# Moving the normalised row-pass input and its mean term from GpSimd to VectorE

## The chip, the cores and the metric

The kernel runs on one core of a Trainium2 chip. The metric is the device time of one execution in microseconds (us). Three runs of the kernel before gave 5276.94, 5283.10 and 5283.75 us, median 5283.1 us. Differences under about 0.2% (10.6 us) can't be told from no change.

## The reference

The input `x` has 8 batches of 128 channels of 128x128 images, float32. Two layers follow each other. Each adds its result to its input, and each first normalises over groups of 4 channels (mean and variance over the 4 images of a group):

```python
def _gn(v, G=32, eps=1e-5):
    g = v.reshape(B_, G, C_ // G, H_, W_)
    m = jnp.mean(g, axis=(2, 3, 4), keepdims=True)
    s = jnp.var(g, axis=(2, 3, 4), keepdims=True)
    return ((g - m) / jnp.sqrt(s + eps)).reshape(v.shape)

x = x + _L0_conv_ref(_gn(x), L0_conv_f)      # per image: upsample by 2 with 12 taps (rows, columns),
                                             # leaky ReLU (slope 0.01), filter and downsample by 2
x = x + _L1_conv_ref(_gn(x), ...)            # rfft2, keep 64x64 modes at both ends, contract with
                                             # four complex factors a, b, c, d, irfft2
```

## The kernel before

Work is cut into quads: the 4 images of one normalisation group, `[128 rows, 4 images, 128 columns]`. There are 256 quads, and four quads make a half, the unit of loading and of the statistics (64 halves). Stage one (`phase1`) does the first layer and the row and column transforms of the second; it fills the first 2840 us of the span. Stages two and three (`phase2`, `phase3`) contract the modes and transform back. The change touches stage one alone.

In stage one every engine runs the same list of steps, one step per quad, each in its own hand-written order, with semaphores between the engines. The loop body has 8 steps (`body`, L605 to L611 on ScalarE, L808 to L814 on VectorE), so the step's place in the half is q mod 4, and after every 32 quads `spectra` is put in. In what follows "place 1" is a step with q mod 4 = 1. At step q:

- TensorE (L385 to L454): `up_cols` of images 0 and 1 (column upsampling, f16 pairs), `down_rows` of quad q-1, at place 2 also `x_sums` (statistics of the next half, L335), then `tails` (L362, the edge columns of both directions; it waits for `e_yb` and `e_yc`), `up_rows` of quad q+1, first half (L324, reads the normalised input `g` and waits for `g_ok`), `up_cols` of image 2 and 3, `up_rows` second half, `down_cols` and `row_transform`.
- ScalarE (L530): copies `L` (slope times the PSUM tile), the high halves of `A`, `Y` and `Z`, and the square root of the variance.
- VectorE (L694): in order `yf(0)`, `yf(1)` (L704, the leaky ReLU as a maximum), `y_tail` (L691, writes `Yc` from the two SBUF tiles `Yt` and `mask`), statistics of `x1b` (L714), the low halves of `Z` and `Zt`, `Ytf`, at place 2 `stats_copy` (L639), `a_low` (L684), `yf(2)`, `yf(3)`, at places 0 and 1 `x_stats` (L632, statistics of two quads of the next half), `a_low` second half, at place 2 `stats_out` (L647, reciprocal of the deviation, `rstd`), and last the new `x1b` (L749).
- GpSimd (L270): high half of `Y` for image 0 (L276), low halves of images 0 and 1 (L283), `Yt` low (L289), at place 2 `variance` (L255), high half of image 2, low halves of images 2 and 3 (L283), and last `ground(q + 2, k + 2, half)` (L240), which makes `g` for quad q+2: `g = x * rstd - nmr`. On the first quad of a half it waits for `rstd` and makes `nmr`, the mean over the deviation, first (L245). `g` has two buffers.

A wait on `e_yc` in `tails` is thus answered by `y_tail`, which is the third instruction of VectorE's step, right behind the last two instructions of its step before (`a_low`, `x1b`).

The lines of TensorE's step on which the argument rests:

```python
if down:
    pe.wait_ge(e_yb, 2 * q)
    pe.wait_ge(e_yc, q)
...
tails(e, o, pr[3], up, down)
if nxt:
    pe.wait_ge(g_ok, q + 2)
    pe.wait_ge(e_yf, 4 * q + 1)
    up_rows(q + 1, k + 1, 0, pr[4])
```

Of the kernel before, what the change touches and what calls it, by code (L numbers as in the profile page):

```python
# [52 lines left out]
def wait(eng, sem, n):  # L53

    if isinstance(n, int) and n <= 0:
        return
    eng.wait_ge(sem, n)  # L57
# [16 lines left out]
def carry(eng, carried):  # L74


    eng.sem_inc(carried, 1)


def phase1(nc, x, ut_d, dt_d, dtail_d, mask_d, dfth_d, dftw_d, ones_d, x1, spec):  # L80
    with ExitStack() as ctx:
# [155 lines left out]

        @block.gpsimd
        def _(pool):
            def ground(q, k, half):  # L240
                if k % HALF == 0:
                    par = k // HALF % 2
                    pool.wait_ge(k_rs, half + 1)
                    carry(pool, carried[0])
                    pool.tensor_tensor(nmr[:, par, :], hm[:], rstd[:, par, :], ALU.mult).then_inc(k_nm, 1)  # L245
                    pool.wait_ge(k_nm, half + 1)
                wait(pool, p_s1, 2 * (q - 1))
                carry(pool, carried[0])
                pool.tensor_scalar(g[:, k % 2].rearrange("p i w -> p (i w)"),  # L249
                                   xb[:, k % SLOTS].rearrange("p i w -> p (i w)"),  # L250
                                   rstd[:, k // HALF % 2, k % HALF:k % HALF + 1],
                                   nmr[:, k // HALF % 2, k % HALF:k % HALF + 1],
                                   ALU.mult, ALU.subtract).then_inc(g_ok, 1)

            def variance(h):  # L255

                pool.wait_ge(k_tot, h + 1)
                carry(pool, carried[0])
                pool.tensor_scalar(hm[:], tot[:, 0], 0.5, None, ALU.mult).then_inc(k_m2, 1)
                pool.tensor_scalar(e2[:], tot[:, 1], 1.0 / 256, None, ALU.mult).then_inc(k_m2, 1)  # L260
                pool.wait_ge(k_m2, 5 * h + 2)
                pool.tensor_tensor(sq[:], tot[:, 0], hm[:], ALU.mult).then_inc(k_m2, 1)
                pool.tensor_tensor(e2[:], e2[:], tot[:, 2], ALU.add).then_inc(k_m2, 1)
                pool.wait_ge(k_m2, 5 * h + 4)
                pool.tensor_tensor(var[:], e2[:], sq[:], ALU.subtract).then_inc(k_m2, 1)
                pool.wait_ge(k_m2, 5 * h + 5)
                carry(pool, carried[0])
                pool.tensor_scalar(var[:], var[:], 0.0, 2 * EPS, ALU.max, ALU.add).then_inc(k_var, 1)

            def step(q, k, half=None):  # L270
                e = k % 2

                def high(m):
                    pool.wait_ge(e_yf, 4 * q + m + 1)
                    carry(pool, carried[0])
                    pool.tensor_copy(Y[:, e, 0, m], Yf[:, m]).then_inc(e_yhp, 1)  # L276

                def low(m):
                    if m % 2:
                        pool.wait_ge(e_yha, 2 * q + m // 2 + 1)  # L280
                    else:
                        pool.wait_ge(e_yhp, 2 * q + m // 2 + 1)
                    pool.tensor_tensor(Y[:, e, 1, m], Yf[:, m], Y[:, e, 0, m], ALU.subtract).then_inc(e_yl, 1)  # L283

                high(0)
                low(0)
                low(1)
                pool.wait_ge(e_yth, q + 1)
                pool.tensor_tensor(Yt[:, e, 1, :], Ytf[:, e, :], Yt[:, e, 0, :], ALU.subtract).then_inc(e_ytl, 1)  # L289
                if half is not None and k % HALF == 2:  # L290
                    variance(half)
                high(2)
                low(2)
                low(3)
                if half is not None:
                    ground(q + 2, k + 2, half)

            def first():
                pool.wait_ge(c_ld, 16 * len(ld_consts))
                variance(0)  # L300
                ground(0, 0, 0)
                ground(1, 1, 0)
                for q in range(4):
                    step(q, q, (q + 2) // HALF)

            def body(t, jq, s6):
                for k in range(8):
                    step(8 * t + 4 + k, k + 4, 2 * t + (6 + k) // HALF)

            def last():  # L310
                for k in range(4):
                    step(252 + k, k + 4, 63 if k < 2 else None)

            steps(pool, first, body, last, lambda: None)
# [310 lines left out]
        def _(dve):  # L625
# [17 lines left out]
            def stats_out(h, par):  # L643
                dve.wait_ge(k_sd, h + 1)
                if not isinstance(h, int) or h >= 2:
                    dve.wait_ge(g_ok, 4 * (h - 1))
                dve.reciprocal(rstd[:, par, :], std[:]).then_inc(k_rs, 1)  # L647

            def batch_in(b):
                dve.wait_ge(b_bn, QUADS * (b + 1))  # L650
# [41 lines left out]
                                  mask[:].unsqueeze(1).to_broadcast(wide), ALU.mult).then_inc(e_yc, 1)  # L692

            def step(q, k, up=True, nxt=True, down=True, rows=True, j5=None, half=None, loads=1, stored=None,  # L694
                     batch=None):


                e, o = k % 2, 1 - k % 2
# [45 lines left out]
                if down:  # L744
                    slot = (k - 1) % SLOTS
                    dve.wait_ge(p_s4, q)
                    if stored is not None:
                        dve.wait_ge(x1_st[stored[0]], 16 * stored[1] + 16)
                    dve.scalar_tensor_tensor(out=x1b[:, slot].rearrange("p i w -> p (i w)"), in0=ring[:, pr[8], 0, :],  # L749
                                             scalar=fac[:, 1:2], in1=xb[:, slot].rearrange("p i w -> p (i w)"),  # L750
                                             op0=ALU.mult, op1=ALU.add).then_inc(e_x1, 1)
                if batch is not None:
                    batch_out(batch, pr[7])

# [17 lines left out]
            def first():  # L772
                dve.wait_ge(c_ld, 16 * len(ld_consts))

                dve.tensor_reduce(fm[:, 0:1], ut[:], AX.X, ALU.max)
                dve.tensor_reduce(fm[:, 1:2], ut[:], AX.X, ALU.min).then_inc(k_f, 1)
                dve.wait_ge(k_f, 1)
                dve.tensor_scalar(fm[:, 2:3], fm[:, 1:2], -1.0, 1e-30, ALU.mult, ALU.max).then_inc(k_f, 1)  # L780
                dve.wait_ge(k_f, 2)
                dve.tensor_tensor(fm[:, 3:4], fm[:, 2:3], fm[:, 0:1], ALU.max).then_inc(k_f, 1)
                dve.wait_ge(k_f, 3)
                dve.reciprocal(fm[:, 4:5], fm[:, 3:4])
                dve.tensor_scalar(fac[:, 0:1], fm[:, 3:4], fm[:, 3:4], 2.0, ALU.mult, ALU.mult).then_inc(k_f, 1)
                dve.wait_ge(k_f, 4)
                dve.tensor_tensor(fac[:, 1:2], fac[:, 0:1], fac[:, 0:1], ALU.mult)
                for t, n in ((ut, 128), (dt, 128), (dtail, TR)):
                    v = dve.tensor_scalar(t[:], t[:], fm[0:n, 4:5], None, ALU.mult)
                v.then_inc(k_f, 1)  # L790
                dve.wait_ge(k_f, 5)
                for t, h_ in ((ut, uth), (dt, dth), (dtail, dtailh)):
                    v = dve.tensor_copy(h_[:, 0, :], t[:])
                v.then_inc(k_f, 1)
                dve.wait_ge(k_f, 6)
                for t, h_ in ((ut, uth), (dt, dth), (dtail, dtailh)):
                    v = dve.tensor_tensor(h_[:, 1, :], t[:], h_[:, 0, :], ALU.subtract)
                v.then_inc(c_up, 1)
                x_stats(0, 1, 0, 0)
                x_stats(0, 1, 0, 1)  # L800
                stats_copy(0, 0)
                stats_out(0, 0)
                a_low(0, 0, 0, pair_of(-1, 4))
                a_low(0, 0, 1, pair_of(-1, 7))
                for q in range(4):
                    step(q, q, down=q >= 1, rows=q >= 2, j5=q - 2, half=1)

            def body(t, jq, s6):  # L808
                for k in range(8):
                    j5 = jq(k) - 1 if s6 is None else (jq(k) - 1) % QUADS  # L810
                    step(8 * t + 4 + k, k + 4, j5=j5, half=2 * t + 2 + k // HALF, loads=t + 2,
                         stored=(1 - k // HALF, t + k // HALF) if k % HALF == 1 else None, batch=s6 if k == 5 else None)
                    if k == 5 and s6 is not None:
                        spectra(s6)  # L814

            def last():
                for k in range(4):
                    step(252 + k, k + 4, nxt=k < 3, j5=26 + k, stored=(1, 31) if k == 1 else None)

            def drain():  # L820
                step(NQ, 0, up=False, nxt=False, j5=30)
# [668 lines left out]
```

## Time and profile before

| | |
|---|---|
| runs, us | 5276.94, 5283.10, 5283.75 |
| span of the profiled execution | 5274.8 us (2.1 to 9.0 us less than the runs) |
| TensorE matmul busy, whole span | 92% |
| VectorE, ScalarE, GpSimd busy | 76%, 65%, 56% |
| `yf` on VectorE (L704) | 1024 instructions, 690.7 us |
| `Y` low halves on GpSimd (L283) | 1024 instructions, 1207.1 us |

The profile is of one execution. A timeline row gives the start of a group of like instructions in us from the start of the span, how long the group took, the engine, the line, the operation and its tiles, the number of instructions, and in brackets the idle time before it with what ended it. PE is TensorE, DVE VectorE, ACT ScalarE, POOL GpSimd. A row by windows gives the stretch in us, its length, the busy us (and instructions) of PE, PEld (weight loads), DVE, ACT and POOL, the granted clock and DMA share, and GB/s. A group row gives line, engine, operation, tiles, count, then busy us and mean ns, then the idle us before with what ended it. An instruction can start up to some hundredths of a us before the printed end of the one ahead of it.

### The profile page before, as it was taken

How to read it: one execution, taken by the hardware profiler on the slowest of the kernel's cores; microseconds unless marked ns; L12 is line 12 of the kernel's file. 1: busy time of each engine (PE TensorE's matmuls, PEld its weight loads, DVE VectorE, ACT ScalarE, POOL GpSimd, SP SyncE). 2: the span in 40 equal slices, each digit the busy share in tenths (PEclk: the TensorE clock that was granted, in tenths of full speed). 3: DMA queues.
4: the chain of work that ended last, by engine and by line, in shares of the span. 5: the costliest groups of instructions: out<-in, count | busy, mean ns of one | idle time of the engine just before them, and what ended most of it. 6: DMA issues, size and time to landing. Idle time of an engine off the chain costs nothing. (4 is left out here: it accounts for less than half of the span.)

```text
span 5274.8 us, 209562 instructions
## 1 busy us (share of the span) xinstructions
PE 4858.2 (92%) x83744; PEld 4311.7 (82%) x83744; DVE 4012.8 (76%) x6181; ACT 3413.0 (65%) x6422; POOL 2969.9 (56%) x3014
## 2 busy tenths in 40 slices
PE   8999999999999999999996689889898998988999
PEld 6888888888888888888886688888888888888999
DVE  6787777877877778778786888888888888883333
ACT  6767767767677677676773566666666666663332
POOL 7968969969689699696991333333333333330000
PEclk9999999999999999999997899999999999999999
DMA  1131131131311311313114122222222222227999
GB/s 53 54 109 55 50 110 54 51 109 54 106 57 51 110 54 50 109 54 106 58 48 146 49 79 76 68 80 64 80 75 68 80 64 80 74 69 307 420 421 398
DMA packets 606585, 553.09 MB, mean 105 GB/s; under 512 B 14900, under 2 KB 540084, under 8 KB 589364
## 3 DMA queue, kind: packets, MB, share of 16 engines
q1 hardware_dynamic: 606132, 546.48, 31.4%
q8 instruction: 354, 5.80, 0.5%
q14 instruction: 99, 0.81, 0.0%
HBM read 277.99 MB, written 268.44 MB: 104 GB/s over the span
## 5 line engine op out<-in xcount | busy, mean ns | idle before, releaser
L1227 DVE TENSOR_TENSOR Ml<-ring,Mh 128x1024 f16<-128x1024 f32 x1024 | 1198.9, 1218 | 201.5 <-ACT Mh L1194 193.6
L283 POOL TENSOR_TENSOR Y<-Yf,Y 128x532 f16<-128x532 f32 x1024 | 1207.1, 1200 | 48.0 <-ACT Y L541 5.1
L1194 ACT ACTIVATE Mh<-ring 128x1024 f16<-128x1024 f32 x1024 | 986.6, 1022 | 301.6 <-PE ring L1128 301.0
L1128 PE MATMUL ring<-wcur,b_hi 64*128 64x128 f16 x16384 | 749.1, 217 | 175.9 <-DVE Ml L1227 136.6
L1128 PEld LDWEIGHTS ring<-wcur,b_hi 64*128 64x128 f16 x16384 | 610.0, 94 | 248.0 <-DVE Ml L1227 154.3
L320 PE MATMUL ring<-uth,A 128*128 128x266 f16 x6144 | 788.6, 277 | 1.0 <-DVE Yf L704 0.5
L704 DVE TENSOR_TENSOR Yf<-ring,L 128x532 f32<-128x532 f32 x1024 | 690.7, 709 | 118.6 <-ACT L L537 94.5
L1128 PE MATMUL ring<-wcur,b_lo 64*128 64x128 f16 x8192 | 715.8, 216 | 0.0
L320 PEld LDWEIGHTS ring<-uth,A 128*128 128x128 f16 x6144 | 599.3, 98 | 137.8 <-issue 3.2
L537 ACT ACTIVATE L<-ring 128x532 f32<-128x532 f32 x1024 | 600.6, 605 | 37.8 <-issue 15.9
L326 PE MATMUL ring<-ut,g 128*128 128x266 f32 x2048 | 576.2, 404 | 50.6 <-POOL g L249 50.6
L684 DVE TENSOR_TENSOR A<-ring,A 128x532 f16<-128x532 f32 x512 | 363.9, 711 | 247.1 <-ACT A L528 241.4
L249 POOL TENSOR_SCALAR g<-xb,rstd,nmr 128x512 f32<-128x512 f32 x256 | 537.6, 2100 | 18.8 <-POOL nmr L245 18.6
L1082 POOL COPY wcur<-w_hi 128x128 f16 (+1 forms) x128 | 37.6, 294 | 869.0 <-PE ring L1128 803.7
L276 POOL CAST Y<-Yf 128x532 f16<-128x532 f32 x512 | 321.2, 627 | 327.9 <-DVE Yf L704 325.4
L1153 PE MATMUL ring<-pout,am 128*128 128x256 f32 x2048 | 477.5, 386 | 8.6 <-DVE pout L1235 0.9
L1141 PE MATMUL ring<-xs,Mh 128*128 128x32 f16 x8192 | 446.0, 177 | 37.9 <-DVE pout L1235 32.8
L1141 PEld LDWEIGHTS ring<-xs,Mh 128*128 128x128 f16 x8192 | 420.4, 96 | 69.0 <-DVE pout L1235 43.8
L326 PEld LDWEIGHTS ring<-ut,g 128*128 128x128 f32 x2048 | 351.3, 191 | 152.2 <-issue 103.5
L541 ACT ACTIVATE Y<-Yf 128x532 f16<-128x532 f32 x512 | 329.0, 643 | 225.8 <-DVE Yf L704 225.0
L1143 PE MATMUL ring<-xs,Ml 128*128 128x16 f16 x8192 | 440.5, 169 | 0.0
L1153 PEld LDWEIGHTS ring<-pout,am 128*128 128x128 f32 x2048 | 380.0, 190 | 72.9 <-DVE pout L1235 19.4
(140 smaller groups left out, 9848.9 us busy)
## 6 DMA issues: line engine op xcount, KB each, us to landing
xb<-in_x SPq DMA_DIRECT2D x128, 512.0 KB, 4.3
x<-x1b SPq DMA_DIRECT2D x64, 1024.0 KB, 6.8
spec<-sp_out SPq DMA_DIRECT2D x256, 256.0 KB, 3.5
xin<-spec SPq DMA_DIRECT2D x128, 512.0 KB, 6.4
fd<-ft SPq DMA_DIRECT2D x128, 512.0 KB, 4.2
F<-fd SPq DMA_DIRECT2D x64, 1024.0 KB, 20.1
xq<-x SPq DMA_DIRECT2D x64, 1024.0 KB, 16.9
out<-yq SPq DMA_DIRECT2D x64, 1024.0 KB, 18.6
```

The source lines that it names most:

```text
L249: pool.tensor_scalar(g[:, k % 2].rearrange("p i w -> p (i w)"), xb[:, k % SLOTS].rearrange("p i w -> p (i w)"), rstd[:, k // HALF % 2, k % ...
L283: pool.tensor_tensor(Y[:, e, 1, m], Yf[:, m], Y[:, e, 0, m], ALU.subtract).then_inc(e_yl, 1)
L320: mm = pe.matmul(out, data(v), const(c), start=(start and n == 0), stop=(stop and n == 2), skip_group_check=True)
L326: mm = pe.matmul(ring[:, pr, m, 0:UPS], g[:, k % 2, 2 * n + m, :], ut[:], start=True, stop=True)
L537: act.activation(L[:, m % 2], ring[:, pr[u], :, 0:UPS], ACT.Copy, scale=SLOPE).then_inc(e_l, 1)
L704: dve.tensor_tensor(Yf[:, m], ring[:, pr[u], :, 0:UPS], L[:, m % 2], ALU.max).then_inc(e_yf, 1)
L1128: mm = pe.matmul(ring[:, UNIT_PAIR[n], t, 128 * k:128 * k + 128], b[r, z, 4 * u + k, :], wcur[r, z, w, :], start=(part == 0), stop=(part = ...
L1141: pe.matmul(o, Mh[:, z, y, :], xs[:, z, y].rearrange("p v r b -> p (v r b)"), start=True, stop=False)
L1143: mm = pe.matmul(o[:, 0:16], Ml[:, z, y, :], xs[:, z, y, 0].rearrange("p r b -> p (r b)"), start=False, stop=True)
L1153: mm = pe.matmul(ring[:, AUX, bank, 256 * z:256 * z + 256], am[:, z, r, C * u:C * u + C], pout[:, z, r, 4 * h:4 * h + 4, :].rearrange("p b ...
L1194: act.activation(hi, ps, ACT.Copy).then_inc(e_hi, 1)
L1227: dve.tensor_tensor(lo, ps, hi, ALU.subtract).then_inc(e_lo, 1)
```

## The change

`ground` goes from GpSimd's step to VectorE's, behind `x1b`; the making of `nmr` goes to VectorE's `stats_out`, right behind the reciprocal that gives `rstd`. The first two `ground` calls move in the same way. `carry` is an increment of a semaphore. The waits of `g` on `p_s1` and on `k_nm` stay; the wait on `k_rs` is now one of VectorE on itself. No tile changes in size, type or number of buffers.

```diff
--- before.py
+++ after.py
@@ -237,21 +237,6 @@
 
         @block.gpsimd
         def _(pool):
-            def ground(q, k, half):
-                if k % HALF == 0:
-                    par = k // HALF % 2
-                    pool.wait_ge(k_rs, half + 1)
-                    carry(pool, carried[0])
-                    pool.tensor_tensor(nmr[:, par, :], hm[:], rstd[:, par, :], ALU.mult).then_inc(k_nm, 1)
-                    pool.wait_ge(k_nm, half + 1)
-                wait(pool, p_s1, 2 * (q - 1))
-                carry(pool, carried[0])
-                pool.tensor_scalar(g[:, k % 2].rearrange("p i w -> p (i w)"),
-                                   xb[:, k % SLOTS].rearrange("p i w -> p (i w)"),
-                                   rstd[:, k // HALF % 2, k % HALF:k % HALF + 1],
-                                   nmr[:, k // HALF % 2, k % HALF:k % HALF + 1],
-                                   ALU.mult, ALU.subtract).then_inc(g_ok, 1)
-
             def variance(h):
 
                 pool.wait_ge(k_tot, h + 1)
@@ -292,14 +277,10 @@
                 high(2)
                 low(2)
                 low(3)
-                if half is not None:
-                    ground(q + 2, k + 2, half)
 
             def first():
                 pool.wait_ge(c_ld, 16 * len(ld_consts))
                 variance(0)
-                ground(0, 0, 0)
-                ground(1, 1, 0)
                 for q in range(4):
                     step(q, q, (q + 2) // HALF)
 
@@ -645,6 +626,20 @@
                 if not isinstance(h, int) or h >= 2:
                     dve.wait_ge(g_ok, 4 * (h - 1))
                 dve.reciprocal(rstd[:, par, :], std[:]).then_inc(k_rs, 1)
+                dve.wait_ge(k_rs, h + 1)
+                carry(dve, carried[1])
+                dve.tensor_tensor(nmr[:, par, :], hm[:], rstd[:, par, :], ALU.mult).then_inc(k_nm, 1)
+
+            def ground(q, k, half):
+                if k % HALF == 0:
+                    dve.wait_ge(k_nm, half + 1)
+                wait(dve, p_s1, 2 * (q - 1))
+                carry(dve, carried[1])
+                dve.tensor_scalar(g[:, k % 2].rearrange("p i w -> p (i w)"),
+                                  xb[:, k % SLOTS].rearrange("p i w -> p (i w)"),
+                                  rstd[:, k // HALF % 2, k % HALF:k % HALF + 1],
+                                  nmr[:, k // HALF % 2, k % HALF:k % HALF + 1],
+                                  ALU.mult, ALU.subtract).then_inc(g_ok, 1)
 
             def batch_in(b):
                 dve.wait_ge(b_bn, QUADS * (b + 1))
@@ -692,7 +687,7 @@
                                   mask[:].unsqueeze(1).to_broadcast(wide), ALU.mult).then_inc(e_yc, 1)
 
             def step(q, k, up=True, nxt=True, down=True, rows=True, j5=None, half=None, loads=1, stored=None,
-                     batch=None):
+                     batch=None, ground_half=None):
 
 
                 e, o = k % 2, 1 - k % 2
@@ -749,6 +744,8 @@
                     dve.scalar_tensor_tensor(out=x1b[:, slot].rearrange("p i w -> p (i w)"), in0=ring[:, pr[8], 0, :],
                                              scalar=fac[:, 1:2], in1=xb[:, slot].rearrange("p i w -> p (i w)"),
                                              op0=ALU.mult, op1=ALU.add).then_inc(e_x1, 1)
+                if ground_half is not None:
+                    ground(q + 2, k + 2, ground_half)
                 if batch is not None:
                     batch_out(batch, pr[7])
 
@@ -800,22 +797,26 @@
                 x_stats(0, 1, 0, 1)
                 stats_copy(0, 0)
                 stats_out(0, 0)
+                ground(0, 0, 0)
+                ground(1, 1, 0)
                 a_low(0, 0, 0, pair_of(-1, 4))
                 a_low(0, 0, 1, pair_of(-1, 7))
                 for q in range(4):
-                    step(q, q, down=q >= 1, rows=q >= 2, j5=q - 2, half=1)
+                    step(q, q, down=q >= 1, rows=q >= 2, j5=q - 2, half=1, ground_half=(q + 2) // HALF)
 
             def body(t, jq, s6):
                 for k in range(8):
                     j5 = jq(k) - 1 if s6 is None else (jq(k) - 1) % QUADS
                     step(8 * t + 4 + k, k + 4, j5=j5, half=2 * t + 2 + k // HALF, loads=t + 2,
-                         stored=(1 - k // HALF, t + k // HALF) if k % HALF == 1 else None, batch=s6 if k == 5 else None)
+                         stored=(1 - k // HALF, t + k // HALF) if k % HALF == 1 else None, batch=s6 if k == 5 else None,
+                         ground_half=2 * t + (6 + k) // HALF)
                     if k == 5 and s6 is not None:
                         spectra(s6)
 
             def last():
                 for k in range(4):
-                    step(252 + k, k + 4, nxt=k < 3, j5=26 + k, stored=(1, 31) if k == 1 else None)
+                    step(252 + k, k + 4, nxt=k < 3, j5=26 + k, stored=(1, 31) if k == 1 else None,
+                         ground_half=63 if k < 2 else None)
 
             def drain():
                 step(NQ, 0, up=False, nxt=False, j5=30)
```

## Rows read from the trace of the kernel before

**Rows 1.** Busy time of each engine in stage one.

```profile
0.00:2840.00 2840.00, 2696.34 (x36384) 2324.08 (x36384) 2235.04 (x3840) 1989.71 (x4362) 2303.22 (x2500) 0.99 0.25 73
```

**Rows 2.** Costliest groups of the page: GpSimd's g, and TensorE's wait for it.

```profile
L249 POOL TENSOR_SCALAR g<-xb,rstd,nmr 128x512 f32<-128x512 f32 x256 | 537.6, 2100 | 18.8 <-POOL nmr L245 18.6
...
L326 PE MATMUL ring<-ut,g 128*128 128x266 f32 x2048 | 576.2, 404 | 50.6 <-POOL g L249 50.6
```

**Rows 3.** Timeline, place 0 into place 1 (step 29).

```profile
306.66 2.36 POOL L283 TENSOR_TENSOR Y<-Yf,Y 128x532 f16<-128x532 f32 x2
...
308.24 0.74 DVE L749 SCALAR_TENSOR_TENSOR x1b<-ring,fac,xb 128x512 f32<-128x512 f32 x1
...
309.10 1.38 DVE L704 TENSOR_TENSOR Yf<-ring,L 128x532 f32<-128x532 f32 x2
...
310.40 0.22 DVE L691 TENSOR_TENSOR Yc<-Yt,mask 40x80 f16<-40x80 f16 x1
...
310.43 0.31 PE L320 MATMUL ring<-dtailh,Yt 40*128 40x20 f16 x6
...
310.88 0.35 PE L320 MATMUL ring<-dth,Yb 128*40 128x64 f16 x6
```

**Rows 4.** Timeline, place 2 (step 30): sums run ahead of the tails.

```profile
319.92 0.22 DVE L691 TENSOR_TENSOR Yc<-Yt,mask 40x80 f16<-40x80 f16 x1
...
320.73 0.36 PE L320 MATMUL ring<-dth,Yb 128*40 128x64 f16 x6
...
321.62 1.16 PE L326 MATMUL ring<-ut,g 128*128 128x266 f32 x4
```

**Rows 5.** Timeline, place 0 into place 1 in other loop bodies (step 13).

```profile
150.94 0.74 DVE L749 SCALAR_TENSOR_TENSOR x1b<-ring,fac,xb 128x512 f32<-128x512 f32 x1
...
151.60 1.32 DVE L704 TENSOR_TENSOR Yf<-ring,L 128x532 f32<-128x532 f32 x2
```

**Rows 6.** Timeline, place 2 into place 3 (steps 30 and 31).

```profile
326.83 2.37 POOL L283 TENSOR_TENSOR Y<-Yf,Y 128x532 f16<-128x532 f32 x2
...
327.45 0.17 DVE L647 RECIPROCAL rstd<-std 128x4 f32<-128x4 f32 x1
...
327.53 0.72 DVE L749 SCALAR_TENSOR_TENSOR x1b<-ring,fac,xb 128x512 f32<-128x512 f32 x1
...
328.49 1.37 DVE L704 TENSOR_TENSOR Yf<-ring,L 128x532 f32<-128x532 f32 x2 [0.23 <-ACT L L537]
...
329.77 0.23 DVE L691 TENSOR_TENSOR Yc<-Yt,mask 40x80 f16<-40x80 f16 x1
...
330.26 0.34 PE L320 MATMUL ring<-dth,Yb 128*40 128x64 f16 x6
...
331.93 1.16 PE L326 MATMUL ring<-ut,g 128*128 128x266 f32 x4 [0.72 <-POOL g L249]
```

**Rows 7.** Timeline, place 3 into place 0 (steps 31 and 32).

```profile
338.79 1.37 DVE L704 TENSOR_TENSOR Yf<-ring,L 128x532 f32<-128x532 f32 x2 [0.29 <-ACT L L537]
```

**Rows 8.** VectorE groups by form: scalar operations from SBUF to SBUF.

```profile
L989 DVE TENSOR_SCALAR am<-am,back 128x1024 f32<-128x1024 f32 x1 | 0.8, 752 | 0.0
...
L960 DVE TENSOR_SCALAR am<-am,alt 128x256 f32<-128x256 f32 x1 | 0.3, 345 | 0.0
```

**Rows 9.** Timeline at the statistics of a batch (step 33).

```profile
355.37 2.43 POOL L283 TENSOR_TENSOR Y<-Yf,Y 128x532 f16<-128x532 f32 x2
...
355.62 1.11 DVE L658 SCALAR_TENSOR_TENSOR sm<-st,sm 128x64 f32<-128x64 f32 x1
```

**Rows 10.** Line L658: ns minimum, median and maximum.

```profile
L658 DVE SCALAR_TENSOR_TENSOR sm<-st,sm x8: 240/1110/1115, 355.6 to 2802.2; 128x64 f32<-128x64 f32 x8
```

**Rows 11.** Timeline behind a spectra stage, GpSimd idle before it.

```profile
390.92 1.32 DVE L704 TENSOR_TENSOR Yf<-ring,L 128x532 f32<-128x532 f32 x2
...
391.79 0.63 POOL L276 CAST Y<-Yf 128x532 f16<-128x532 f32 x1 [31.89 <-DVE Yf L704]
...
392.16 0.35 DVE L691 TENSOR_TENSOR Yc<-Yt,mask 40x80 f16<-40x80 f16 x1
```

## The prediction

> **What bounds the kernel now.** I read the busy time by stage first. In stage one TensorE is busy 2696 of 2840 us (95%), GpSimd 2303 (81%), VectorE 2235 (79%) [rows 1]. So TensorE sets the pace, 144 us of it are gaps, and what counts is which wait makes each gap. The page names one that the change is aimed at: TensorE waited 50.6 us in all for GpSimd's `g` [rows 2]. It comes once in each half, at place 3, where `g` must wait for `rstd`: from the tails to `up_rows` there are 1.67 us (330.26 to 331.93), where a step without this wait has 0.89 (320.73 to 321.62), so 0.78 us a half [rows 4, 6].
>
> The second gap is not in the list by name, because it is short. I looked for it step by step in the timeline. At place 1 `Yc` ends at 310.62, TensorE's matmuls ahead end at 310.74, and the tails start at 310.88, 0.26 us behind `Yc` [rows 3]. The same 0.26 (330.00 to 330.26) is there at place 3 [rows 6]. I went through all steps: at places 1 and 3 all but three of 126 steps show it, of the 63 at place 0 some 48 do (all 31 in the second half of the loop body, 17 of 32 in the first half, where TensorE is held elsewhere). Other latencies vary from step to step; so TensorE is waiting for VectorE's `Yc` there, and anything that delays it costs TensorE time one for one. At place 2 it is 0.59 (320.14 to 320.73), as the sums stand between: a slack of 0.33 [rows 4]. VectorE is idle 21% of the stage, but between `x1b` and `Yc` nearly not: `yf(0)` starts 0.12 us behind `x1b`'s end at places 1 and 2 [rows 3], 0.24 at place 3 [rows 6], 0.29 at place 0 [rows 7], and 0.08 ahead of its printed end in about half of the loop bodies at place 1 (back to back) [rows 5]. Just there the change puts its instruction.
>
> **The price of `g` on VectorE.** The trace has no such instruction of 512 elements. The same kind takes 752 ns for 1024 elements and 345 ns for 256 [rows 8], so 0.53 ns an element and 0.48 us for 512; with its second scalar per partition I take 0.50. The ends are 0.48 and the 0.74 us that `x1b`'s form with one element a cycle takes for 512 [rows 3]; I take the near end because kind and tiles are the same. The Trainium skill (VectorE: DVE Perf Modes, The TRN2 errata) gives 58 cycles plus half the elements at 0.96 GHz for this form, an estimate of 0.33 us; the trace's own rows are longer, and by 0.33 the loss worked out below would be about 30 us in place of 47.
>
> Back to back it starts 0.08 ahead of `x1b`'s printed end, so it ends 0.42 behind that, and `yf(0)` can start at +0.34. Against the idle time above, `yf(0)` comes later by 0.22 at places 1 and 2, by 0.42 in the bodies without idle time, and by 0.05 at place 0 (0 in the first half of the body).
>
> **Two instructions that share a path.** VectorE and GpSimd hold each other up here. `sm` (L658), with two SBUF inputs, takes 240 ns when GpSimd is idle, and 1110 when it starts under GpSimd's `Y` subtraction [rows 10]. It started at 355.62, the first of GpSimd's two ended about 356.60, `sm` at 356.73: held until GpSimd's instruction was over, let in between two of them, done 0.13 behind [rows 9]. Three things follow.
> - `Yc` has two SBUF inputs. Now GpSimd makes `g` while it runs, and it takes its 0.22. When `g` is gone, GpSimd starts its copy of `Y` right behind `yf(0)`, as it does today behind spectra, and there `Yc` takes 0.35: `yf(0)` to the end of `Yc` is 1.59 us [rows 11] in place of 1.52 [rows 3]. +0.07 in each step, +0.14 in the tight bodies.
> - `nmr` (two SBUF inputs, 0.16 us alone as small neighbours; the 0.17 of the reciprocal is the row nearest to it) is wanted at 327.65. GpSimd runs two subtractions from 326.83 to 329.20, the first to about 328.02 [rows 6]. `nmr` ends at 328.10 and not 327.81, and `x1b` behind it at 328.75 in place of 328.25.
> - `g` itself has one SBUF input. Nothing in the trace shows such an instruction under a GpSimd one, so its hold lies between 0 and the rest of the GpSimd instruction. Its 0.53 ns an element is two elements a cycle where `x1b` does one; it must be reading by two paths like `sm`, so I take it as held. At places 0, 1 and 3 GpSimd's last subtraction ends 0.04 behind `x1b` (309.02, 308.98) [rows 3], inside `g`'s start-up: no cost. At place 2 `g` is wanted at 328.67 and held to 329.20, so it ends at 329.57 (0.50 less the 0.13 of start-up behind the release), and `yf(0)` starts at 329.49 against 328.49.
>
> The Trainium skill says the same of the last case (SBUF — State Buffer, Who interferes with whom): a single-source VectorE instruction in a two-port mode takes the pair of ports it shares with GpSimd for its whole length, and whoever starts second is blocked. By it the sum is mine; without it for `g`, see the third rival.
>
> **The sum, for 8 steps.** Delay of the tails:
> - Place 1: 0.22 + 0.07 = 0.29 in the one half of the body; in the other a mean of 0.29 and 0.42 + 0.14 = 0.56, 0.43. Together 0.72.
> - Place 2: 0.28, inside the 0.33 of slack: 0, twice.
> - Place 3: 1.00, and 1.59 in place of 1.51 (328.49 to 330.00) to the end of `Yc` [rows 6], 1.08 later; and the 0.78 wait for `g` goes, since `g` ends long before: +0.30, twice, 0.60.
> - Place 0: 0.05 + 0.07 = 0.12; in the first half of the body 0.07 in half the cases, 0.04. Together 0.16.
>
> That is 1.48 us in 8 steps, and 32 times 8 steps give 47 us. Small things: the first `g` of the kernel comes 1.6 us earlier (2.10 less 0.50 [rows 2]); `batch_out` behind `g` is up to 0.42 later 8 times, 3 us at most; some steps around the 8 spectra stages have more slack. They cancel to within 3 us. GpSimd loses 537.6 us of work [rows 2], and nothing else waits for it: the halves of `Y` it makes late today are used a step later. The added waits on VectorE have nothing to wait for but the reciprocal just ahead; queued behind them are `x1b` and `yf(0)`, counted above.
>
> The span 5274.8 becomes 5322; the median of the runs lies 8.3 above the span, so 5283 + 47 = **5330 us**.
>
> **Rivals.**
> 1. Faster. VectorE's idle fifth absorbs `g` and `nmr`: the 0.26 behind `Yc` is then a fixed latency of the tails themselves, and only the wait for `g` counts. All 50.6 us less what is at the start go: 64 times 0.78 is 50, so 5234. For it: the named wait [rows 2]. Against: the 0.59 and larger values where TensorE is busy. 16%.
> 2. Neither `nmr` nor `g` is held. Then `yf(0)` at place 3 starts at 328.80, with `Yc` +0.38, less 0.78: -0.40, twice. The sum is 1.48 - 1.40 = 0.08, times 32, +3: 5286, no change. Against: `sm`. 12%.
> 3. `nmr` is held, `g` is not. `yf(0)` at 329.09: 0.67 less 0.78 is -0.11, the sum 0.66, +21: 5304. 10%.
> 4. Dearer, slower than my forecast. GpSimd doesn't let VectorE in between its two subtractions: `nmr` waits to 329.20, `yf(0)` starts at 330.24, place 3 costs 1.04 in place of 0.30, +47 more: 5377. Or `g` runs at one element a cycle, 0.74 us: places 1, 0 and 2 then cost 0.24 more each (less the slack at place 2), place 3 0.13, a sum of 2.4, +76: 5359. Together 12%.
>
> My forecast holds 50%. The turn between gain and loss is place 3: if its tails come less than 0.78 - 0.44 = 0.34 us later, the change pays; 0.44 is what the other places cost a half.
>
> **How the numbers follow.** Faster by over 0.2% is the first rival, 0.16. Within 0.2% is the second, 0.12. Slower is the rest, 0.72. The likeliest case alone is 5305 to 5350 (0.48 to 0.58 us for `g`, half of the tight bodies either way). The range to 5378 takes in the fourth rival, the lower end 5270 leaves out the first: 5270 to 5378.
>
> **What would show it.** `g` on VectorE at 0.48 to 0.52 us at places 0, 1 and 3, about 0.9 at place 2; `nmr` about 0.45 and not 0.16; `Yc` at 0.35 in nearly all steps; from the tails at place 2 to those at place 3 about 10.6 us in place of 9.53 (320.73 to 330.26) [rows 4, 6]; the distance from the tails to `up_rows` at place 3 down from 1.67 to 0.89; GpSimd's busy time down by 538 us. I am wrong if the tails don't start 0.26 behind `Yc` any more, or if `g` at place 2 is as short as elsewhere.

## The result and the profile after

The changed kernel takes 5324.6 us in the median of four runs (5314.6 to 5327.5), the kernel before 5280.7 (5276.9 to 5283.8). The ratio is 1.0072 with a 95% interval of 1.0057 to 1.0086: slower by 38 us by the ratio, 44 by the medians. Forecast were 5330 and +47. The profiled spans are 5325.4 and 5274.8 us. Of all the runs in this document one, of e9, fell into a slow state (6074.3 us at a granted clock of 0.75 where its others had 0.98), and the ratios leave it out.

The busy time of stage one over the same 2840 us, to be read beside [rows 1] (PE, PEld, DVE, ACT, POOL, then the granted clock):

```profile
0.00:2840.00 2840.00, 2657.72 (x35980) 2288.21 (x35981) 2365.05 (x4105) 1978.52 (x4334) 1776.10 (x2176) 0.99 0.24 70
```

TensorE did less in the same stretch (the changed kernel is not as far at 2840 us), VectorE 130 us more, GpSimd 527 us less: the work was moved as meant. The page's groups of `g` and of TensorE's row pass answer to [rows 2] (lines have moved: `g` is L638 now, `up_rows` L307):

```profile
L638 DVE TENSOR_SCALAR g<-xb,rstd,nmr 128x512 f32<-128x512 f32 x256 | 157.6, 616 | 0.1
```

```profile
L307 PE MATMUL ring<-ut,g 128*128 128x266 f32 x2048 | 578.6, 406 | 4.1 <-DVE g L638 4.0
```

TensorE's wait for `g` went from 50.6 us to 4.1, and those are one wait at the start, before the first quad. What took its place is named by the instructions' own view, line `y_tail` (L686): duration in ns, minimum, median and maximum, and who waited for it.

```profile
L686 DVE TENSOR_TENSOR Yc<-Yt,mask x256: 290/352/974, 35.0 to 2843.0; 40x80 f16<-40x80 f16 x128
...
  PE ring L301: 123.5, 168
```

`Yc` takes 352 ns in the median where it took 223, and TensorE's idle time that it ended is 123.5 us in 168 steps; in the kernel before the same view counted 13.4 us in 10.

The timeline of place 0 into place 1, second half of the loop body (compare [rows 3]):

```profile
352.11 0.74 DVE L744 SCALAR_TENSOR_TENSOR x1b<-ring,fac,xb 128x512 f32<-128x512 f32 x1
...
352.76 0.54 DVE L638 TENSOR_SCALAR g<-xb,rstd,nmr 128x512 f32<-128x512 f32 x1
...
353.22 1.32 DVE L699 TENSOR_TENSOR Yf<-ring,L 128x532 f32<-128x532 f32 x2
...
354.09 0.63 POOL L261 CAST Y<-Yf 128x532 f16<-128x532 f32 x1 [1.21 <-DVE Yf L699]
...
354.46 0.35 DVE L686 TENSOR_TENSOR Yc<-Yt,mask 40x80 f16<-40x80 f16 x1
...
355.07 0.34 PE L301 MATMUL ring<-dth,Yb 128*40 128x64 f16 x6 [0.30 <-DVE Yc L686]
```

`g` stands where `yf(0)` used to start. `yf(0)` begins 0.37 us behind `x1b`'s end (352.85), GpSimd's copy begins right behind `yf(0)`, `Yc` starts under it and takes 0.35, and the tails begin 0.26 behind `Yc` (354.81 to 355.07): the same distance as before, now with a wait of 0.30 that the profile names.

Place 2 into place 3 (compare [rows 6]):

```profile
331.31 2.36 POOL L268 TENSOR_TENSOR Y<-Yf,Y 128x532 f16<-128x532 f32 x2
...
331.93 0.17 DVE L628 RECIPROCAL rstd<-std 128x4 f32<-128x4 f32 x1
332.25 0.28 DVE L631 TENSOR_TENSOR nmr<-hm,rstd 128x4 f32<-128x4 f32 x1 [0.15 <-DVE rstd L628]
...
332.44 0.74 DVE L744 SCALAR_TENSOR_TENSOR x1b<-ring,fac,xb 128x512 f32<-128x512 f32 x1
...
333.11 0.84 DVE L638 TENSOR_SCALAR g<-xb,rstd,nmr 128x512 f32<-128x512 f32 x1
...
333.87 1.32 DVE L699 TENSOR_TENSOR Yf<-ring,L 128x532 f32<-128x532 f32 x2
...
335.11 0.35 DVE L686 TENSOR_TENSOR Yc<-Yt,mask 40x80 f16<-40x80 f16 x1
...
335.71 0.35 PE L301 MATMUL ring<-dth,Yb 128*40 128x64 f16 x6 [1.16 <-DVE Yc L686]
...
336.60 1.16 PE L307 MATMUL ring<-ut,g 128*128 128x266 f32 x4
```

The tails now wait 1.16 us for `Yc`. From the tails to `up_rows` there are 0.89 us (335.71 to 336.60): the wait for `g` is gone.

From such timelines of the whole stage I took two distances for each of the 8 positions in the loop body, 0 to 7 (place is the position modulo 4): the gap from the end of TensorE's `Yt` matmuls to the start of the tails (-0.07 where nothing is waited for; medians of 31 or 32 steps, of two middle values the larger), and, for place 3, tails to `up_rows`. Sum is the mean distance of the tails added over 8 positions, so 32 sums are the stage.

```
                        gap ahead of the tails, us                 tails to     sum of
kernel                  pos 1   pos 3   pos 4   pos 5   pos 7      up_rows, 3   8 steps
before                  0.15    0.14    0.14    0.14    0.14       1.68         86.84
changed                 0.74    1.12    0.30    0.30    1.13       0.88         88.41
e1 g alone              0.71    1.72    0.29    0.30    1.71       0.88         90.66
e2 mean alone           0.15    0.23    0.14    0.14    0.24       1.06         86.70
e3 copy after yf(1)     0.61    0.99    0.17    0.30    0.99       0.88         87.74
e4 short subtraction    0.71    0.81    0.29    0.30    0.81       0.88         88.05
e5 before, Yc first    -0.07   -0.07   -0.07   -0.07   -0.07       1.83         86.14
e6 changed, Yc first   -0.07   -0.07   -0.07   -0.07   -0.07       0.90         84.78
e7 g behind Yc          0.15    0.14    0.14    0.14    0.14       0.88         86.03
e8 e7, Yc first        -0.07   -0.07   -0.07   -0.07   -0.07       1.06         85.34
e9 e7, no wait          0.23    0.22    0.23    0.22    0.23       0.88         86.64
```

Positions 2 and 6 have 0.47 in every kernel (the sums stand between), position 0 has -0.07 (-0.05 in the kernel before). The changed kernel's sum is 1.57 us longer, times 32 is 50 us, about the difference of the spans (50.6).

The median hides one thing: with `g` behind `x1b`, position 1 has two kinds of bodies. In the changed kernel 20 of 32 have a gap of 0.58 to 0.75 and 12 one of 0.23 to 0.39; the mean is 0.58, against 0.14 in the kernel before. Sums of time go by the mean.

### The profile page after: what moved, and what is told of

Its sections match the earlier page's. It is cut to its first block and busy times, and to the rows that moved or that the text cites. A ratio compares the mean times of both kernels' runs of the same rounds, so it can differ in the third digit from the quotient of the medians.

```text
span 5325.4 us, 209314 instructions
## 1 busy us (share of the span) xinstructions
PE 4861.9 (91%) x83744; PEld 4315.4 (81%) x83744; DVE 4179.3 (78%) x6501; ACT 3419.1 (64%) x6422; POOL 2447.1 (46%) x2694
## 3 DMA queue, kind: packets, MB, share of 16 engines
q14 instruction: 129, 1.06, 0.1%
## 5 line engine op out<-in xcount | busy, mean ns | idle before, releaser
L307 PE MATMUL ring<-ut,g 128*128 128x266 f32 x2048 | 578.6, 406 | 4.1 <-DVE g L638 4.0
L301 PE MATMUL ring<-dth,Y 128*128 128x64 f16 (+1 forms) x12288 | 422.6, 194 | 24.4 <-issue 18.1
L301 PEld LDWEIGHTS ring<-dth,Y 128*128 128x128 f16 x12288 | 409.9, 97 | 38.9 <-issue 21.1
```

The costliest lines, as they stand in the source:

```text
L301: mm = pe.matmul(out, data(v), const(c), start=(start and n == 0), stop=(stop and n == 2), skip_group_check=True)
L307: mm = pe.matmul(ring[:, pr, m, 0:UPS], g[:, k % 2, 2 * n + m, :], ut[:], start=True, stop=True)
```

## The experiments

The edits below are shown short. Those of e2 and e5 are against the kernel before, all others against the changed kernel. The kernel before was run beside each group of kernels: 5284.2 us in the median beside e1 to e4, 5284.4 beside e5 to e8, 5283.8 beside e9.

**e1: `g` alone moved.** The mean over the deviation stays on GpSimd.

```diff
-                dve.wait_ge(k_rs, h + 1)
-                dve.tensor_tensor(nmr[:, par, :], hm[:], rstd[:, par, :], ALU.mult).then_inc(k_nm, 1)
+                if half is not None and k % HALF == 2:       # end of GpSimd's step
+                    mean_over(half, (k + 2) // HALF % 2)     # waits k_rs, makes nmr, k_nm
```

> One part alone: g is made by VectorE behind x1b as in the changed kernel, the mean over the deviation (nmr) by GpSimd at the end of its step as before. Theory (VectorE's chain x1b, g, yf(0), yf(1), Yc sets TensorE's tails): at place 2 the g waits for GpSimd's nmr, which comes after the last subtraction (0.9 us behind x1b's end), so yf(0) starts some 1.6 us behind x1b's end in place of 0.69, while x1b itself comes 0.43 earlier; the tails at place 3 come about 0.6 us later than in the changed kernel, 64 times, +37 us: 5362 us. Rival (the moved mean is what costs, g is hidden in VectorE's idle time): about 5281, the time of the kernel before, or less.

Measured: 5392.7 us, ratio 1.0204 (1.0187 to 1.0221), 68 us more than the changed kernel. The expected part is there: the gap at place 3 is 1.72 in place of 1.12, 0.60 as forecast, or 38 us. The timeline shows the chain, from GpSimd's last subtraction over `nmr` to `g` and the tails:

```profile
342.57 2.36 POOL L273 TENSOR_TENSOR Y<-Yf,Y 128x532 f16<-128x532 f32 x2
...
344.88 0.21 POOL L258 TENSOR_TENSOR nmr<-hm,rstd 128x4 f32<-128x4 f32 x1
...
345.28 0.55 DVE L643 TENSOR_SCALAR g<-xb,rstd,nmr 128x512 f32<-128x512 f32 x1 [1.28 <-POOL nmr L258]
...
347.59 0.34 PE L309 MATMUL ring<-dth,Yb 128*40 128x64 f16 x6 [1.73 <-DVE Yc L691]
```

The time lies 31 us over the 5362 forecast, and these do not show in that gap: see the clock below. The rival (5281 or less) is out.

**e2: the mean alone moved.** `nmr` on VectorE, `g` on GpSimd, whose `ground` waits for `k_nm` in place of `k_rs`.

```diff
-                    pool.wait_ge(k_rs, half + 1)
-                    pool.tensor_tensor(nmr[:, par, :], hm[:], rstd[:, par, :], ALU.mult).then_inc(k_nm, 1)
                     pool.wait_ge(k_nm, half + 1)
+                dve.wait_ge(k_rs, h + 1)                     # behind the reciprocal
+                dve.tensor_tensor(nmr[:, par, :], hm[:], rstd[:, par, :], ALU.mult).then_inc(k_nm, 1)
```

> The other part alone: nmr is made by VectorE behind the reciprocal, g stays on GpSimd. Theory: x1b at place 2 comes about 0.43 us later, of which the 0.24 of idle time ahead of yf(0) takes half, the tails at place 3 come 0.2 later; GpSimd's g starts at once behind its last subtraction, 0.4 to 0.5 us earlier than before, and TensorE's wait for it (0.78 us) shrinks to about 0.15 behind the later tails: 0.45 us a half, 64 times, -28 us: 5253 us. Rival (whatever is added to VectorE there is lost one for one and the wait for g is hidden elsewhere): 5281 or up to 13 us more.

Measured: 5256.7 us, ratio 0.9946 (0.9929 to 0.9963): this half of the change is a gain of 27 us. The tails at place 3 come 0.09 later (0.20 forecast), and the distance to `up_rows` falls from 1.68 to 1.06; together 0.53 a half, 34 us. The sum in the table shows only 4 us of it: the profiled run was the slowest of the four (5272.1 us, the others 5253.8 to 5258.0), and it holds seven pauses of TensorE's own, 13.3 us, that the kernel before doesn't have (below).

**e3: GpSimd's first copy waits for `yf(1)`.**

```diff
-                    pool.wait_ge(e_yf, 4 * q + m + 1)
+                    pool.wait_ge(e_yf, 4 * q + max(m, 1) + 1)
```

> The changed kernel, but GpSimd starts its first copy of Y behind yf(1) in place of yf(0), so that Yc starts ahead of it. Theory (Yc's 0.35 us is 0.13 of waiting for GpSimd's copy): Yc is back at 0.22, the tails come 0.13 earlier at places 0, 1 and 3, five of eight steps: 0.13 x 5 x 32 = 21 us less than the changed kernel, 5304. GpSimd's lateness is taken up by its wait for Yt. Rival (Yc is longer for a reason of its own): 0.35 stays and the time is 5325; rival (GpSimd's halves come too late): the time rises.

Measured: 5303.3 us, ratio 1.0038 (1.0025 to 1.0050), 21 less than the changed kernel, as forecast. `Yc`:

```profile
L686 DVE TENSOR_TENSOR Yc<-Yt,mask x256: 220/223/971, 35.9 to 2822.1; 40x80 f16<-40x80 f16 x128
```

Its median is back at 223 ns, so the 0.13 were a wait for GpSimd's copy. The gap at place 3 shrinks by 0.13, at positions 4 and 1 by the same; at position 5 it stays at 0.30. So four positions gain and not five, 17 us; that the time meets the forecast to the us is luck.

**e4: GpSimd's last subtraction of place 2 cut to one column in each part** (that low half of `Y` is left stale).

```diff
+                    n = 1 if m == 3 and k % HALF == 2 else UPS
-                    pool.tensor_tensor(Y[:, e, 1, m], Yf[:, m], Y[:, e, 0, m], ALU.subtract).then_inc(e_yl, 1)
+                    pool.tensor_tensor(Y[:, e, 1, m, :, 0:n], Yf[:, m, :, 0:n], Y[:, e, 0, m, :, 0:n], ...)
```

> The changed kernel, but GpSimd's last subtraction of each half's place 2 (Y low of image 3) works on one column of 266 in each of the two parts: that low half is left stale. Theory (g at place 2 is held until GpSimd's subtraction is over): g takes 0.54 there in place of 0.84, the tails at place 3 start 0.30 earlier, 64 times, 19 us less: 5306. Rival (g is longer there because of the nmr and x1b ahead of it, not because of GpSimd): 0.84 stays, 5325.

Measured: 5311.1 us, ratio 1.0046 (1.0028 to 1.0064), 13.5 less than the changed kernel. `g` at place 2 is back at its free price:

```profile
334.49 0.53 DVE L640 TENSOR_SCALAR g<-xb,rstd,nmr 128x512 f32<-128x512 f32 x1
```

The gap at place 3 falls from 1.12 to 0.81, the 0.31 that `g` was held. That is 20 us; the time fell by some 6 us less than that and than the forecast 19, and this profile has seven of TensorE's own pauses (14.4 us) where the changed kernel's has three (6.4 us).

**e5: the kernel before with `Yc` made first**, and **e6: the changed kernel with `Yc` made first.** The edit is the same in both:

```diff
+                if down:
+                    y_tail(o, q)
                 if up:
                     yf(0, 0)
                     yf(1, 1)
-                if down:
-                    y_tail(o, q)
```

> The kernel before, but VectorE makes Yc at the head of its step, ahead of yf(0), in place of behind yf(1). Theory (the tails start 0.26 us behind Yc because they wait for it): at places 1 and 0 the tails start up to 0.21 us earlier, right behind TensorE's matmuls; at place 3 up_rows still waits for GpSimd's g and nothing is won. Three of eight step positions, 0.21 x 3 x 32 = 20 us less: 5264. Rival (0.26 is a latency of the tails themselves and Yc was never waited for): 5284, unchanged.

> The changed kernel with Yc made ahead of yf(0). Theory (the whole loss of the change is TensorE's wait for Yc): the waits ahead of the tails (0.74 at place 1 and 0.30 at place 0 or 1 of the other half body, 1.12 at place 3, each counted from the matmuls ahead, where an unstalled step has -0.07) go away, 3.9 us in eight steps, at most 126 us less than the changed kernel, if nothing else is late next: 5200 to 5220, under the kernel before. Rival (VectorE's load as such slows the step, the place of Yc doesn't matter): 5325 less at most 10.

Measured: e5 5255.6 us, ratio 0.9939 (0.9919 to 0.9958); e6 5206.7 us, ratio 0.9845 (0.9825 to 0.9864). These two decide the first rival of the prediction. With `Yc` early the 0.26 behind it is gone and TensorE runs through: it was a wait. In e5, at the step of [rows 3]:

```profile
306.74 0.22 DVE L691 TENSOR_TENSOR Yc<-Yt,mask 40x80 f16<-40x80 f16 x1
...
307.99 0.31 PE L320 MATMUL ring<-dtailh,Yt 40*128 40x20 f16 x6
...
308.23 0.36 PE L320 MATMUL ring<-dth,Yb 128*40 128x64 f16 x6
```

The forecast for e5 was 20 us less. The sums give 22, the profiled spans 20.5 (5274.8 to 5254.3), the medians of the runs 29; e6 lies inside its forecast of 5200 to 5220. And with this one wait out of the way the change turns from a loss of 44 us into a gain of 49 (5255.6 to 5206.7). Timeline of e6, place 3 into place 0:

```profile
1014.70 0.54 DVE L638 TENSOR_SCALAR g<-xb,rstd,nmr 128x512 f32<-128x512 f32 x1
...
1015.15 0.23 DVE L686 TENSOR_TENSOR Yc<-Yt,mask 40x80 f16<-40x80 f16 x1
1015.30 1.32 DVE L699 TENSOR_TENSOR Yf<-ring,L 128x532 f32<-128x532 f32 x2
...
1015.90 0.31 PE L301 MATMUL ring<-dtailh,Yt 40*128 40x20 f16 x6
...
1016.14 0.36 PE L301 MATMUL ring<-dth,Yb 128*40 128x64 f16 x6
...
1017.04 1.17 PE L307 MATMUL ring<-ut,g 128*128 128x266 f32 x4
```

`Yc` ends at 1015.38, 0.76 us ahead of the tails, and the tails start at 1016.14, before the printed end of the `Yt` matmuls (1016.21).

**e7: `g` at another place of VectorE's step**, behind `Yc`, for the next quad; `nmr` on GpSimd as in e1; GpSimd's first copy of `Y` waits for this `g`. **e8** is e7 with `Yc` first.

```diff
                 if down:
                     y_tail(o, q)
+                if ground_half is not None:
+                    ground(q + 1, k + 1, ground_half)
...
-                if ground_half is not None:
-                    ground(q + 2, k + 2, ground_half)
...
+                    if m == 0:                               # GpSimd's high(0)
+                        pool.wait_ge(g_ok, q + 2)
```

> g on VectorE at another place: behind Yc and ahead of the statistics, where VectorE waited 0.6 us for Z, for the row pass that TensorE begins behind the tails; nmr stays on GpSimd; GpSimd's first copy of Y waits for this g, so that it doesn't hold it. Theory (only the place between x1b and Yc costs): x1b, yf(0), yf(1), Yc are as in the kernel before, Yc is 0.22 and g 0.54 everywhere, the wait of 0.78 us for g is gone, 64 times: 50 us less than before, 5233. Rival (VectorE's total load costs, wherever g stands): about 5300 or more.

> The kernel of e7 with Yc made ahead of yf(0) as well. Theory: the wait for g (0.78 us a half) and the waits for Yc (0.21 us at five of eight step positions) are both gone: 50 + 34 = 84 us less than the kernel before, 5200. Rival: what is late next (g itself, which now ends only 0.5 us ahead of its row pass) takes the second part back: 5233.

Measured: e7 5248.9 us, ratio 0.9926 (0.9907 to 0.9946); e8 5217.1 us, ratio 0.9862 (0.9838 to 0.9886). VectorE's load is that of the changed kernel less `nmr` (0.27 us a half), and the time is under that of before: the place costs, not the load. e7 misses its 5233 by 16 us though its gaps are all as expected; its profile has seven of TensorE's own pauses, 15.2 us in all (below). e8 misses its 5200 by 17 us, as it starts from e7: it gets 32 of the 34 us more that it was to get over e7. But `g` ends too late for place 3 (1.06 in place of 0.90), which is why e6 is the better of the two.

**e9: e7 without GpSimd's wait for `g`.**

```diff
-                    if m == 0:
-                        pool.wait_ge(g_ok, q + 2)
```

> The kernel of e7 (g behind Yc), but GpSimd's first copy of Y no longer waits for g, so GpSimd runs its copy and its subtraction (1.2 us) there. Theory (VectorE's g, with one SBUF input, is held for the rest of a GpSimd instruction): Yc takes 0.35, g is caught behind the subtraction and takes about 1.5 us in place of 0.53; the statistics and Z behind it start some 0.9 us late, yf(2) and the next Yc with them: about 0.5 to 0.7 us a step, 130 to 180 us more than e7: 5380 to 5430. Rival (the 0.84 of g at place 2 in the changed kernel was something else): g stays at 0.53, the time at 5249 or some 20 us more for Yc.

Measured: 5273.6 us, ratio 0.998 (0.9969 to 0.9992). My forecast of 5380 or more is wrong, and so is its mechanism in this place. One step:

```profile
1015.01 0.63 POOL L266 CAST Y<-Yf 128x532 f16<-128x532 f32 x1 [1.18 <-DVE Yf L704]
1015.43 0.31 DVE L691 TENSOR_TENSOR Yc<-Yt,mask 40x80 f16<-40x80 f16 x1
...
1015.66 0.53 DVE L643 TENSOR_SCALAR g<-xb,rstd,nmr 128x512 f32<-128x512 f32 x1
1015.72 1.52 POOL L273 TENSOR_TENSOR Y<-Yf,Y 128x532 f16<-128x532 f32 x1
```

```profile
L643 DVE TENSOR_SCALAR g<-xb,rstd,nmr x256: 529/530/1410, 19.0 to 2773.2; 128x512 f32<-128x512 f32 x128
```

`g` starts 0.06 us ahead of GpSimd's subtraction and takes its 0.53; the subtraction takes 1.52 in place of 1.20, in 249 of 256 steps. The hold goes both ways, and the one that comes first is not held. GpSimd had time to spare, so in the step only `Yc` (0.31) was dearer, 0.08 at five positions, 13 us. The time is 25 us over that of e7; the records of the granted clock show the low level for 65 us up to 2740 us, where e7 has 41; half of the 24 more is an estimate of the rest, and no run shows it alone. The time is near the rival's 5269, but its reason (`g` was never held) is not what the rows show: e4 speaks against it. That the outcome turned on 0.06 us I had not seen when I forecast.

## Why the prediction was right

The step that carried it, TensorE waits for `Yc` though the list of waits hardly says so, is shown by e5 and e6. From the tails at place 2 to those at place 3 there are 10.5 us in the mean, forecast 10.6. Point by point, in us:

- **Price of `g`**: 0.54 against 0.50 forecast. `yf(0)` starts 0.37 behind `x1b`, forecast 0.34.
- **`Yc` under GpSimd's copy**: 0.35 in the median, as forecast; e3 shows the cause.
- **`g` held at place 2**: shown by e4. It takes 0.84 (333.11 to 333.95), forecast about 0.9.
- **`nmr` held**: mis-sized. It took 0.27 and not 0.45, since it starts 0.32 behind the reciprocal and not 0.20, nearly at the end of GpSimd's first subtraction. The sum was hardly hurt: `x1b` starts 0.51 behind the reciprocal, 0.43 more than before, forecast 0.50. In its place stands VectorE's wait for its own result.
- **Place 3**: gap +0.98, `up_rows` wait -0.80, net +0.18 to +0.19 (by the means +0.95 and +0.98, -0.77, net 0.39 for both halves); forecast +1.08 and -0.78, net +0.30, 0.60 for both.
- **Place 2**: no cost, as forecast. `Yc` to tails fell from 0.59 to 0.43.
- **Place 0**, second half of the body: +0.16, forecast +0.12.
- **Place 1**: in the first half of the body the mean gap grew by 0.44, forecast 0.43: the tight bodies by 0.60 (0.56 forecast), the others by 0.1 to 0.25. In the second half of the body it grew by 0.16 in place of 0.29, and that is the term that was off.
- **GpSimd's busy time**: down by 523 over the whole span (2969.9 to 2447.1), forecast 538.
- **The loss if `g` took 0.33**: a mis-sum. The prediction's own terms, each with 0.17 less, give some 24 us and not 30. Nothing else used it.

The 0.16 of the second half has a reason in the rows. I had taken `yf(2)` to hang on TensorE's `up_cols` behind the tails. It hangs on `Z`, which hangs on `down_rows` ahead of the tails. In the kernel before, `yf(2)` comes 3.70 us behind the tails:

```profile
340.56 0.34 PE L320 MATMUL ring<-dth,Yb 128*40 128x64 f16 x6
...
341.52 1.23 DVE L718 TENSOR_TENSOR Z<-ring,Z 128x1024 f16<-128x1024 f32 x1 [0.61 <-ACT Z L555]
...
344.26 1.33 DVE L704 TENSOR_TENSOR Yf<-ring,L 128x532 f32<-128x532 f32 x2 [0.25 <-ACT L L537]
```

In the changed kernel it is 3.54:

```profile
345.39 0.34 PE L301 MATMUL ring<-dth,Yb 128*40 128x64 f16 x6 [0.30 <-DVE Yc L686]
...
346.19 1.23 DVE L713 TENSOR_TENSOR Z<-ring,Z 128x1024 f16<-128x1024 f32 x1 [0.45 <-ACT Z L536]
...
348.93 1.33 DVE L699 TENSOR_TENSOR Yf<-ring,L 128x532 f32<-128x532 f32 x2
```

`Z` starts 0.96 behind the tails in the one and 0.80 in the other, and `yf(2)` comes 2.74 behind `Z` in both (by way of `Ytf`, ScalarE's `Yt` and its `L`). A stall of the tails doesn't move `Z`, so behind a stalled step VectorE's chain starts 0.16 us earlier as TensorE counts. At position 5 the chain from `x1b` to `Yc` is 0.24 + 0.08 = 0.32 longer, starts 0.16 earlier, and 0.16 is left. This reading rests on the rows; no run undid it alone.

**The account.** By the means, gaps and waits in eight steps changed by 0.44 + 0.18 (place 1), 0.39 (place 3, two waits for `g` off), 0.19 (place 0) and -0.07 (place 2): 1.13, times 32 is 36 us. The stage grew by 50. The other 14 us are at the head of the loop body. TensorE's pauses of over 1 us with no releaser ("issue") are 0 in the kernel before and 3, 6.4 us in all, in the changed one; and the granted clock is at its low level for 41 us in place of 24 up to 2740 us. So two errors of opposite sign, the places too dear by 11 us (47 forecast, 36 found) and the loop head not thought of, met in a sum that is right to 3 us; the sign and the mechanism are well supported, the closeness is luck.

## What to carry to other kernels

A wait that comes in every step and lasts 0.2 us hides from the list of waits; look for a distance between two engines' instructions that is the same in every step (0.26 us here), and take it away by order before you load the chain that feeds it. A short instruction that another engine waits for (`Yc`, 0.22 us, its inputs ready long before) belongs at the head of the step, not behind 1.3 us of others: that alone was 20 us by the profiled spans (29 by the medians), and it turned the moved work from -44 to +49 us. A median over steps of two kinds hides one kind: 0.74 was the median at position 1, 0.58 the mean, and a sum of time wants the mean. And the head of the loop body can hide what an experiment of this size is to show: e4 missed by 6 us and e7 by 16 with all their gaps as expected. When work goes from one engine to its neighbour, check what the first now does at the freed time, and whom that holds up.

## What the runs showed of the hardware

**VectorE and GpSimd hold each other up in both directions.** VectorE's single-input scalar operation on 128x512 f32 in SBUF takes 0.54 us free, 0.84 when GpSimd's subtraction is ahead of it (e4 takes this away), and stretches that subtraction from 1.20 to 1.52 when it is ahead itself (e9). The Trainium skill (SBUF — State Buffer, Who interferes with whom) says that the first to start takes the shared pair for its whole length. These runs agree that the second is held, by 0.30 where `g` lay 0.56 us under the subtraction and by 0.32 where the subtraction lay 0.47 us under `g`. But `Yc` (two SBUF inputs) took 0.22 in the kernel before while GpSimd's own `g`, 2.1 us with one SBUF input, ran across it; only GpSimd's copy (0.35) and subtraction (1.12 at place 3 of e5) held it. The section makes no exception for such a GpSimd instruction, so here the measurement differs from it, and I can't say why.

**TensorE pays for a pause twice.** In e7 the head of a loop body shows a pause that no engine ended, and slow matmuls behind it:

```profile
296.52 1.30 PE L311 MATMUL ring<-dth,Y 128*128 128x69 f16 x20 [2.39 <-issue]
...
299.44 2.14 PE L317 MATMUL ring<-ut,g 128*128 128x266 f32 x4
...
301.38 2.36 PE L311 MATMUL ring<-uth,A 128*128 128x266 f16 x12
...
303.57 1.06 PE L317 MATMUL ring<-ut,g 128*128 128x266 f32 x4
```

```profile
292.00:296.40 4.40, 2.13 (x40) 1.83 (x37) 3.76 (x7) 2.19 (x6) 1.88 (x4) 0.98 0.02 4
296.50:303.50 7.00, 6.98 (x54) 5.05 (x55) 2.47 (x4) 3.46 (x7) 2.95 (x3) 0.53 0.01 2
303.60:310.00 6.40, 6.26 (x113) 5.60 (x111) 5.92 (x11) 4.22 (x10) 2.98 (x3) 1.00 0.07 19
```

After 2.39 us of pause the four `up_rows` matmuls take 2.14 us where they take 1.16, the granted clock is 0.53 for 7 us (the 1.2 GHz level for most of it) and then 1.00 again. Such stretches, counted by groups of four `up_rows` matmuls that take over 1.6 us, are 7 in the kernel before, 8 in the changed one and 23 in e1, where 15 of them stand right behind tails that waited 1.72 us at place 3. The granted clock is at the low level for 102 us of e1 up to 2740 us, for 41 of the changed kernel. If matmuls take twice as long there, the 61 us more are an estimate of up to 31 us lost, the 31 us that e1's forecast missed; no run changed the clock alone.

**The pauses at the head of the loop body.** TensorE's own, over 1 us, are 0 in the kernel before, 3 in the changed one, 5 in e1 and 6 to 9 in e2 to e9 (10 to 18 us a run); in e7 they are 7, 15.2 us in all. The kernel before is not free of pauses either. In six bodies ScalarE stands still for 2.5 to 2.8 us with no releaser, and it reaches TensorE through `yf(0)` and `Yc`:

```profile
1116.65 0.61 ACT L537 ACTIVATE L<-ring 128x532 f32<-128x532 f32 x1 [2.55 <-issue]
...
1119.24 0.35 PE L320 MATMUL ring<-dth,Yb 128*40 128x64 f16 x6 [2.14 <-DVE Yc L691]
```

Such pauses of ScalarE, six a run, are in all eleven kernels. In the kernel before, the waits for `Yc` behind them are 12.5 of the 13.4 us that the view of `Yc` counted. Why an engine pauses at the head of the loop body, and why TensorE does so more often in every edited kernel than in the kernel before, stays open: no run changed only that. Each kernel has one profile, so how far the pauses differ from run to run isn't known either.
